# An attention kernel's order of work: shift two groups behind the scores, transposes of the maxima inside the second key block's scores, the values' product in one go a pair, exponential a bank at a time

## The reference

```
x = x + layernorm(attention(layernorm(x)))
x = x + layernorm(ffn(layernorm(x)))
attention: q, k, v = linear(x), 16 heads of 16
  qk = q k^T / sqrt(16) + sum_d q[l,d] * rel_emb[r - l + 511, d]
  out = linear(softmax(qk) v)
ffn: base linear + rank-16 shared expert + 6 rank-16 routed experts,
  of which the two with the largest gates count, weighted by their gates
```

## Time and profile before

| | |
|---|---|
| three runs | 6338.6, 6333.1, 6343.19 us; median 6338.6 |
| the profiled execution's own time | 6342.86 us |
| its span | 6341.1 us |
| TensorE's mean granted clock over the span | 0.985 of full |
| busy of ScalarE, GpSimd | 49%, 58% |
| DMA | 296.74 MB, mean 47 GB/s |

### The profile page before, as it was taken

The page is one execution under the profiler, slowest core; times in us unless marked ns, Lnnn a source line. Parts: engine busy times, 40 slices in busy tenths (PEclk is TensorE's granted clock), DMA queues, the critical chain, the costliest instruction groups (busy, mean ns, idle before and its releaser), DMA issues.

```text
span 6341.1 us, 408511 instructions
## 1 busy us (share of the span) xinstructions
PE 5961.8 (94%) x178176; PEld 5617.6 (89%) x178176; DVE 4987.0 (79%) x10289; ACT 3127.8 (49%) x5145; POOL 3652.9 (58%) x4709
## 2 busy tenths in 40 slices
...
GB/s 87 39 44 52 36 61 36 54 44 38 60 36 62 36 36 62 36 61 34 42 58 36 60 37 49 47 40 60 36 53 45 36 60 40 59 37 36 62 36 27
DMA packets 570090, 296.74 MB, mean 47 GB/s; under 512 B 384177, under 2 KB 534689, under 8 KB 568625
## 3 DMA queue, kind: packets, MB, share of 16 engines
...
...
## 4 chain that ended last, share of the span: by engine, by line
PE 83%; DVE 8%; issue 4%; DVEq 3%; POOLq 1%; ACT 1%; POOL 0%; SPq 0%; DMA 0%
PE sc L667 22%; PE pw L693 15%; PE sc L683 14%; PE sc L662 13%; PE pm L714 4%; PE pw L700 4%; PE pw L714 4%; PE pm L674 4%; DVE r L962 3%; DVEq L973 2%; DVE y2n L928 2%; DVE nm L971 1%; PE pm L727 1%; PE pm L705 1%; DVE gate L1005 1%
## 5 line engine op out<-in xcount | busy, mean ns | idle before, releaser
L962 DVE TRANSPOSE_TENSOR_REDUCE r<-sc 128x32 f16<-128x1024 f32 x2048 | 2548.8, 1245 | 52.0 <-PE sc L667 51.4
L667 PE MATMUL sc<-rm,tw 96*128 96x32 f16 x65536 | 2293.4, 177 | 71.6 <-issue 70.8
L847 ACT ACTIVATE prob<-sc 128x1024 f32<-128x1024 f32 x2048 | 2097.3, 1024 | 193.7 <-PE sc L683 141.3
L667 PEld LDWEIGHTS sc<-rm,tw 96*128 96x128 f16 x65536 | 1979.9, 97 | 79.5 <-issue 79.0
L662 PE MATMUL sc<-qm,ks 96*128 96x64 f16 x32768 | 1639.8, 193 | 28.8 <-DMA ks<-qk_s 15.5
L971 DVE TENSOR_REDUCE nm<-pm 16x32 f16<-16x256 f32 x2048 | 840.8, 411 | 753.7 <-PE pm L674 750.3
L662 PEld LDWEIGHTS sc<-qm,ks 96*128 96x128 f16 x32768 | 1302.8, 98 | 34.3 <-issue 34.2
L683 PE MATMUL sc<-nmm,pick 128*128 128x64 f16 x32768 | 1302.0, 193 | 2.5 <-DVE nmm L974 1.2
L683 PEld LDWEIGHTS sc<-nmm,pick 128*128 128x128 f16 x32768 | 1151.9, 98 | 122.4 <-issue 105.5
L693 PE MATMUL pw<-prob,vs 128*32 128x128 f32 x32768 | 1115.7, 277 | 129.8 <-DVE nm L971 124.7
L693 PEld LDWEIGHTS pw<-prob,vs 128*32 128x32 f32 x32768 | 842.6, 110 | 185.8 <-DVE nm L971 137.4
...
## 6 DMA issues: line engine op xcount, KB each, us to landing
...
tw<-tw_s SPq DMA_DIRECT2D x512, 72.0 KB, 2.1
...
```

The lines of the kernel that those rows point to most:

```text
L667: last = mm(out3[:, :, 2 * k:2 * k + 2], tw[:, jp, u:u + P], rm[:, i, k, :, :], start=False, stop=False, skip_group_check=True)
L847: A(prob[:, jp % 2, :, :, i * IW:(i + 1) * IW], sc[:, 2 * buf:2 * buf + 2, :].rearrange("p c (h i) -> p c h i", i=IW), ACT.Exp).then_inc(s ...
L962: v.tensor_reduce(r1[:, 0:2 * H], sc[:, 2 * buf:2 * buf + 2, :].rearrange("p c (h i) -> p (c h) i", i=IW), axis=AX.X, op=ALU.max, apply_tr ...
```

## The change

LAG = 2: group g now begins with `wide` and `mixed`, then come content and relative products of the first block, the shift of group g - 2 (it was g - 1, after everything else), the content products of the second block, the transposes of the maxima of group g - 1, and the relative products of the second block. `scores` is split into `content` and `rel`. The values' product runs whole at k = 3 (it was half at k = 1 and half at k = 2), the transposes of the parts move to k = 0 of the next pair, the projections from k = 0 to k = 1. In `pm`, the transposed maxima of the pair move from k = 1 to k = 2 and into the last 16 columns (`p_nm`), and some of the products move by one group (0 to 1, 8 to 9). The wait on s_nmr, now for group g - 2, stands only ahead of groups that write `pm`. ScalarE's exponential is two instructions, one a bank, and s_exp counts both; the wait for a free buffer is now one for each bank. On VectorE `maxima` of group g - 1 comes first, then `side`, then `spread` of group g - 1; `side` has the combination at g = 3 (it was 1) and the softmax division at g = 8 (it was 7).

```diff
--- before.py
+++ after.py
@@ -28,6 +28,8 @@
 NH = NA + E
 EPS = 1e-5
 NBUF = 3
+LAG = 2
+MIXED = (1, 3, 9, 10, 11, 12)
 def buffer(t, g):
@@ -185,6 +187,7 @@
         p_max = pm[:, 0:2 * P]
         p_n = pm[:, 2 * P:3 * P]
         p_t = pm[:, 2 * P:4 * P]
+        p_nm = pm[:, 4 * P - H:4 * P]
         s_const = sem("s_const")
@@ -652,16 +655,20 @@
             pe.wait_ge(s_cpool, 1)
             pe.wait_ge(s_cdve, 1)
-            def scores(g, c, buf):
+            def content(g, c, buf):
                 jp, i = divmod(g, NI)
                 bank = sc[:, 2 * buf + c, :]
-                out3 = bank.rearrange("p (h i) -> p h i", i=IW)
                 j = (2 * jp + c) * P
                 for h in range(H // 2):
-                    last = mm(bank[:, 2 * h * IW:(2 * h + 2) * IW], ks[:, h, j:j + P],
-                              qm[:, i, 2 * h:2 * h + 2, :].rearrange("p h i -> p (h i)"),
-                              start=(h == 0), stop=False, skip_group_check=True)
+                    mm(bank[:, 2 * h * IW:(2 * h + 2) * IW], ks[:, h, j:j + P],
+                       qm[:, i, 2 * h:2 * h + 2, :].rearrange("p h i -> p (h i)"),
+                       start=(h == 0), stop=False, skip_group_check=True)
+            def rel(g, c, buf):
+                jp, i = divmod(g, NI)
+                out3 = sc[:, 2 * buf + c, :].rearrange("p (h i) -> p h i", i=IW)
                 for k in range(IW // 2):
                     u = P - 1 - (i * IW + 2 * k) + c * P
                     last = mm(out3[:, :, 2 * k:2 * k + 2], tw[:, jp, u:u + P], rm[:, i, k, :, :],
@@ -684,9 +691,9 @@
                                   start=False, stop=True, skip_group_check=True)
                 last.then_inc(s_shift, 1)
-            def pv(jp, half):
-                for col in (2 * half, 2 * half + 1):
+            def pv(jp):
+                for col in range(4):
                     for c in range(2):
                         for q in range(4):
                             h = 4 * col + q
@@ -718,16 +725,10 @@
                 return [(lambda i, c=c: lhs[:, i, c, cols], lambda j, c=c: rhs[:, j, c, :]) for c in range(2)]
-            def mixed(t, g, att, a, b):
-                jp, k = divmod(g, NI)
-                if k == 1 and (a if jp == 0 else att):
-                    mm(p_n[:, 0:H], nm[:, (jp - 1) % 2, :], ident16[:, 0:H], start=True, stop=True)\
-                        .then_inc(s_nmtp, 1)
-                    return s_nmt, t * NJP + jp
-                if g == 0 and b:
+            def mixed(t, g, a, b):
+                if g == 1 and b:
                     pe.wait_ge(s_xn1, t - 1)
                     transpose2(p_t, xn1).then_inc(s_x1Tp, 1)
                     return s_x1T, t - 1
@@ -736,7 +737,7 @@
                     pe.wait_ge(s_x1T2, t - 1)
                     product(p_t[:, 0:NH], *both(x1T2, w_a2)).then_inc(s_hp, 1)
                     return s_hf, t - 1
-                if g == 8 and a:
+                if g == 9 and a:
                     pe.wait_ge(s_o, t)
                     transpose2(p_t, o[:, :, :].rearrange("p h d -> p (h d)")).then_inc(s_oTp, 1)
                     return s_oT, t
@@ -758,24 +759,11 @@
             def wide(t, n, g, att, proj, a):
                 jp, k = divmod(g, NI)
-                if k and (a if jp == 0 else att):
-                    pj = (jp - 1) % NJP
-                    if k == 1:
-                        pe.wait_ge(s_exp, t * NG + g - 1)
-                        pe.wait_ge(s_vs[pj], batch_of(t - 1 if jp == 0 else t) * 16 + 16)
-                        if proj and jp < 3:
-                            pe.wait_ge((s_xT, s_qkf, s_vf)[jp], n + 1)
-                        else:
-                            pe.wait_ge(s_part, t * NJP + jp - 1)
-                        pv(pj, 0)
-                    elif k == 2:
-                        pv(pj, 1).then_inc(s_pv, 1)
-                    else:
-                        transpose_parts(t * NJP + jp - 1)
-                if k == 0 and jp < 3 and proj:
-                    if a if jp == 0 else att:
+                if k == 0 and (a if jp < 2 else att):
+                    transpose_parts(t * NJP + jp - 2)
+                if k == 1 and jp < 3 and proj:
+                    if a if jp < 2 else att:
                         pe.wait_ge(s_part, t * NJP + jp - 1)
                     elif jp == 0:
                         pe.wait_ge(s_vf, n)
@@ -792,12 +780,29 @@
                     else:
                         pe.wait_ge(s_qkf, n + 1)
                         product(pw[:, 0:D], *both(xT2, w_v2)).then_inc(s_vp, 1)
+                if k == 3 and (a if jp == 0 else att):
+                    pj = (jp - 1) % NJP
+                    pe.wait_ge(s_exp, t * (2 * NG) + 2 * NI * jp)
+                    pe.wait_ge(s_vs[pj], batch_of(t - 1 if jp == 0 else t) * 16 + 16)
+                    if proj and jp < 3:
+                        pe.wait_ge((s_xT, s_qkf, s_vf)[jp], n + 1)
+                    else:
+                        pe.wait_ge(s_part, t * NJP + jp - 1)
+                    pv(pj).then_inc(s_pv, 1)
             def tile(t, n, att, proj, a, b, ph=None):
                 read = None
                 for g in range(NG):
                     jp, k = divmod(g, NI)
-                    old = a if g == 0 else att
+                    turned = k == 2 and (a if jp == 0 else att)
+                    wide(t, n, g, att, proj, a)
+                    if (turned or g in MIXED) and (a if g < LAG else att):
+                        pe.wait_ge(s_nmr, t * NG + g - 1)
+                    read = mixed(t, g, a, b)
+                    if turned:
+                        mm(p_nm, nm[:, (jp - 1) % 2, :], ident16[:, 0:H], start=True, stop=True).then_inc(s_nmtp, 1)
+                    buf = buffer(ph, g) if att else None
                     if att:
                         if k == 0:
                             pe.wait_ge(s_tw[jp], t * 16 + 16)
@@ -805,26 +810,25 @@
                         if jp == 0:
                             pe.wait_ge(s_mask, t * NI + k + 1)
                         free = t * NG + g - NBUF + 1
-                        if not (isinstance(free, int) and free <= 0):
-                            pe.wait_ge(s_exp, free)
-                        scores(g, 0, buffer(ph, g))
+                        taken = not (isinstance(free, int) and free <= 0)
+                        if taken:
+                            pe.wait_ge(s_exp, 2 * free - 1)
+                        content(g, 0, buf)
+                        rel(g, 0, buf)
+                    if a if g < LAG else att:
+                        shift(buffer(ph, g - LAG), t * NG + g - 1)
+                    if att:
+                        if taken:
+                            pe.wait_ge(s_exp, 2 * free)
+                        content(g, 1, buf)
                     if read is not None:
                         pe.wait_ge(*read)
-                    if old:
+                    if turned:
+                        pe.wait_ge(s_nmt, t * NJP + jp)
+                    if a if g < 1 else att:
                         transpose_max(t * NG + g)
                     if att:
-                        scores(g, 1, buffer(ph, g)).then_inc(s_scores, 1)
-                    wide_first = k == 1 or g in (0, 8)
-                    if wide_first:
-                        wide(t, n, g, att, proj, a)
-                    if old:
-                        pe.wait_ge(s_nmr, t * NG + g)
-                    read = mixed(t, g, att, a, b)
-                    if not wide_first:
-                        wide(t, n, g, att, proj, a)
-                    if old:
-                        shift(buffer(ph, g - 1), t * NG + g)
+                        rel(g, 1, buf).then_inc(s_scores, 1)
             passes(pe, tile)
@@ -844,14 +848,15 @@
                 act.wait_ge(s_shift, count)
                 if not (isinstance(free, int) and free <= 0):
                     act.wait_ge(s_pv, free)
-                A(prob[:, jp % 2, :, :, i * IW:(i + 1) * IW],
-                  sc[:, 2 * buf:2 * buf + 2, :].rearrange("p c (h i) -> p c h i", i=IW),
-                  ACT.Exp).then_inc(s_exp, 1)
+                for c in range(2):
+                    A(prob[:, jp % 2, c, :, i * IW:(i + 1) * IW],
+                      sc[:, 2 * buf + c, :].rearrange("p (h i) -> p h i", i=IW), ACT.Exp).then_inc(s_exp, 1)
             def before(g, t, ph):
-                pg = (g - 1) % NG
-                exp(pg, buffer(ph, g - 1), t * NG + g, (t - 1 if g == 0 else t) * NJP + pg // NI - 1)
+                pg = (g - LAG) % NG
+                exp(pg, buffer(ph, g - LAG), t * NG + g - LAG + 1,
+                    (t - 1 if g < LAG else t) * NJP + pg // NI - 1)
             def tile(t, n, att, proj, a, b, ph=None):
                 for g in range(NG):
@@ -860,12 +865,21 @@
                     pj = (jp - 1) % NJP
                     old = a if jp == 0 else att
-                    if k == 1 and old:
+                    if k == 2 and old:
```

(44 more changed lines are left out.)

## The result

The changed kernel takes 6973.07 us (median of 4 runs, 6956.22 to 6978.39) against 6339.07 us before: a ratio of 1.0996, with a 95% interval from 1.0974 to 1.1018. The forecast had the sign and part of the mechanism, but its 6627 us and the upper end of its range, 6850, are too low.

The account below looks back on a forecast made before the run. It took VectorE's chain to bind groups with little extra TensorE work: 48.1 + 1.0 (VectorE against GpSimd) + 1.35 (lg blocked) = 50.45 us a tile against 48.2, 288 us more, so 6627 us; range 6310 to 6850.

Parts of the forecast that it names:

- VectorE's chain: From one transposes of the maxima to the next: VectorE needs 2.24 us, binding groups with under 0.39 us extra TensorE work.
- lg behind L583: Router's lg falls behind GpSimd's large product in group 4, by a 0.2 us margin, ending at 3.6: +1.35 us a tile.
- Skewing the work: TensorE's side work by group: k = 2 left with 0.04 us, k = 3 given 1.92; the sixteen intervals sum to 47.54.
- rival 4: GpSimd blocks VectorE in more places, group 9's expert weights and nmm of groups 2 and 5: 6851 us, chance 0.15.
- the row: Forecast's table of intervals between transposes for iterations 0 to 15, with lg's 0.79 and 0.96 us put into 5 and 6.
- The gate: Gate's side work on VectorE, about 3.2 us from the maxima, makes its interval 2.87 us.
- The wait on s_nmr charged at nothing: TensorE's new wait at k = 2 lies inside VectorE's 2.24 us, so it was given no cost.
- The back edge: Wait called issue before L667, taken for the loop's back edge: 0.55 us a tile, which stays.
- The hole: Values' product in one go saves one of two holes after weight changes: 0.2 us a pair, about 104 us.
- The exponential: ScalarE's exponential a bank at a time, 0.6 us each, is covered by slack: cost taken as 0.
- The shift two behind: With the shift two groups behind, the wait on nmm, no more than a trace, goes.
- the faster case: Rival: TensorE stays the bound and side work finds more cover, 46.3 us a tile, 6096 us; chance 0.14.

Follow-up runs that it names:

- e2: Changed kernel with GpSimd's three operations of the combination cut to 17 elements, so the attention's output is not computed: 6556.73 us (one run).
- e1: Changed kernel with 20 products into an idle bank ahead of the wait on s_nmr in groups 6 and 10: 6780.29 us.
- e9: Kernel before the change with the whole values' product at k = 2 and nothing wide at k = 1: 6740.76 us.
- e6: Changed kernel with GpSimd's combination waiting until lg is made and its split of oT until hw is made: 6704.12 us.
- u1: Changed kernel with the exponential of both banks in one instruction again: 6986.83 us.
- u2: Changed kernel with the transposes of the maxima ahead of the second block's content products again: 6759.88 us.
- e8: Changed kernel with values' product in halves, maxima's transposes ahead of the second block's content products, and GpSimd's split of oT behind the expert weights: 6341.31 us.

## Why the prediction was right in sign and short in size

**VectorE's chain: right.** Iterations 4, 8, 9, 12, 13, 14 and 15 came out within 0.1 us of the forecast, 3 within 0.2. Group 13, without TensorE work, does fall only to VectorE's 2.24.

**lg behind L583: right.** 1.85 us in the timeline; I had "ends at 3.6", that is 2.0. The price was too small: +1.35 a tile with all set off, while e2 measured 3.23, of which 0.98 in interval 7 is the clock and a part L591's. The Trainium skill, page "SBUF — State Buffer", section "Who interferes with whom", says that a VectorE instruction with two inputs in SBUF contends with a GpSimd one that reads SBUF, and that the order of issue decides which of them is blocked. The trace agrees: lg, which started 0.21 us after L583, ended 0.02 us after it. The margin of 0.2 us that I gave was 0.21.

**The step that failed: "Skewing the work".** It priced the product in one go at 1.92 us wherever it stood, which is right at full clock (1.89). The sum has no term for TensorE's clock. In the changed kernel the product of groups 7 and 11 runs at half clock in more than half of the tiles because TensorE stood still in the groups before, and e1 shows the size: 1.82 us a tile in intervals 7 and 11, and 193 us net. The same step in the kernel before (e9) gives 6.93 us for one interval.

**The second miss: the blocks in group 9.** I had them in rival 4 with a chance of 0.15, and the sum without them. They are there (swn 652, hw 687 ns), interval 10 is 0.87 over the forecast, and e6, which removes them, brings it to 2.63. Together: 50.45 + 1.05 + 0.93 + 0.87 = 53.3, what was measured. That it fits so well is in part luck: the other thirteen intervals are 1.2 above the row, beside the 1.15 that the sum has and the row leaves out (1.0 and 0.55, less 0.4), and errors of both signs are in them (5 and 6).

**The gate: too large, which hid a part.** I took its 3.2 us from the kernel before, where cgt took 1.15 because it started behind GpSimd's L549. In the changed kernel cgt is free (197 ns), and interval 6 came out 0.48 under the forecast. The 0.92 us less of cgt are more than that gap.

**The wait on s_nmr charged at nothing: right for the sum as far as is seen, wrong in its effect.** It is inside VectorE's chain as long as only time counts, but it is one of the places where TensorE stands (162.2 + 158.4 us at L804 and L750), and so costs clock.

**Iterations 0 to 2** are longer than the forecast's row by 1.04 together. L979 takes 0.37, 0.35 and 0.54 us there in the mean, 0.72 more than three free ones, and TensorE's wait called issue before L674 is 33.0 us in 44 times, 0.26 a tile. These are the size of the gap; no run shows that they are it. The back edge, which I had as staying at 0.55, is less.

**The hole: smaller than taken.** The whole product lasts 1.89, two halves 2.04, so 0.15 a pair or 77 us, not 104. That the halves at k = 1 have the same hole was right; in the kernel before the weight load of L727, behind them, waits 102.5 us in 512 times, 0.2 each.

**The exponential: right** (u1). **The shift two behind: wrong.** I wrote that the wait on nmm goes. It grew from 1.2 to 70.9 us, in the iteration behind lg, where L979 comes late. **The place of the transposes: no term for it in the sum.** In u2 the eight products ahead of them decide on which side of L583 lg falls: 213 us. The lag by itself was not tried alone.

**Rivals.** Nothing speaks for the faster case: e8, which keeps the shift two behind and has lg, swn and hw unblocked and a clock of 0.991, only comes level with the kernel before. Rival 4, blocks in more places, was nearest with its 6851; it has no term for the clock either. Of what was to prove me right: TensorE idle at L681, L804 and L750 did come (395 us, 3.1 a tile), lg at some 2 us too; but VectorE's idle share rose to 26%, where I had forecast a fall, since it in turn waited 1282.7 us for L681 (750.3 before) at the slow product.

What stays open: how much of iterations 0 to 2 belongs to the masks of GpSimd, which run there and which no experiment moved.
